# Local attention on one core: keys normalised first, the queries' norm moved into the masking instruction, and the projection copies issued before the fourth exponential

## The chip, the core and the metric

One core of a Trainium2 chip runs the whole program in one launch. The metric is device time in microseconds (us), taken as the median of a few executions; one further execution was recorded by the hardware profiler. All lines (L1134 and so on) are lines of the kernel before, unless the text says otherwise.

## The reference, cut to what matters

The program is a chain of four blocks on an input of 2 batches of 2048 tokens with 256 channels: causal attention, a quantised linear layer, a second causal attention, and then two layers of *local attention followed by a feed-forward network*. Only local attention is touched:

```python
qkv = shift_token(x) @ wqkv              # 256 -> 3 x 512, 8 heads of 64
q, k = l2norm(q) * qs, l2norm(k) * ksc   # each head's vector over its length
q, k = rotary_xpos(q, k)                 # x * cos + rotate_half(x) * sin, per position
# 16 windows of 128 tokens; a window's queries see its own keys and those of the window before
sim = einsum(8 * q, k); sim = where(mask, -big, sim)
x = x + (softmax(sim) @ v) @ wo
```

The norm of a query is one number per token and head, so it can be multiplied in before the scores are made or after. The tables of cosines and sines are ready in SBUF when the stage begins.

## The kernel before, in words

`local_attention` (L1134 to L1484) runs four times in an execution: 2 batches by 2 layers. Each run works through 16 windows of 128 tokens (`w`), and in each window through 4 pairs of heads (`p`); `n = 4w + p` numbers the 64 pairs. Each engine has its own instruction list, written out by hand, and runs it strictly in that order; semaphores (`S[...]`) join the lists. While window `w` is attended, window `w+1` is projected, rotated, normalised and transposed.

- **TensorE** (L1178 to L1281). For each pair: `scores` (L1217), then work for the window ahead, then `turn_p(n-1)` (L1225, transposes of the probabilities of the pair before) and `pv(n-2)` (L1237, probabilities times values). The work ahead is: at p = 0 `turn_h` (L1187) and the projections of queries and keys (L1197); at p = 2 the projection of values; at p = 3 first `out(w-1)` (L1252, the output projection) and then `turn_qk(w+1)` (L1206), which transposes the normalised queries `qn` and keys `kn` into the PSUM banks BQ and BK.
- **ScalarE** (L1283 to L1356). `exp(n)` (L1320) for each pair; at p = 0 `h_out` and the squares of both projections (L1300); at p = 2 `v_take`; at p = 3, after `exp(n)`, `qk_out(w+1)`: the copy of the transposed queries (L1308) and two copies of the keys into their block layout (L1314). Then `p_out(n-1)` (L1326), and at p = 1 `o_out(w-1)` (L1330).
- **VectorE** (L1382 to L1483). `maximum` (L1437, adds the mask to the scores, writes them out and takes the row's extreme), `scale` (L1446 reciprocal, L1449 multiplication), and for the window ahead `squares` (L1399 sum, L1402 clamp), `rotate` (L1415 cosine part, L1418 sine part), `normalise` (L1427, product with the inverse norm, for `qn` and `kn`) and `add` (L1455).
- **GpSimd** (L1358 to L1380). For queries and then keys: the inverse norm as a power (L1376, 128 x 8 values), and the sum of the cosine and sine parts (L1378, in place in `prod_cos`). In layer 0 it also keeps a copy of x (L1371).

The first scores of a window wait for both copies of its keys (L1213), so TensorE can't begin window `w+1` before `qk_out(w+1)` is done. `PROJECTED` (L1147) says at which pair each projection is issued, for TensorE and ScalarE alike.

Of the kernel before, what the change touches and what calls it, by code (L numbers as in the profile page):

```python
# [25 lines left out]
P = 128  # L26
# [1107 lines left out]
def local_attention(k, l, x2, F, keep):  # L1134
# [7 lines left out]
              "sq_q sq_k rot_q rot_k sumsq sum_q sum_k inv_n qn kn q_T k_T q_T_out k_T_out scored maxed exped rinv pn "  # L1142
# [4 lines left out]
    PROJECTED = ((0, 1), (), (2,), ())  # L1147
    with ExitStack() as ctx:
# [7 lines left out]
        ssum, inv_n, mhalf = sb("ssum", [P, 2 * LH]), sb("inv_norm", [P, 2 * LH]), sb("mhalf", [P, 2 * LH])  # L1156
        qn, kn = sb("qn", [P, INNER]), sb("kn", [P, INNER])
# [12 lines left out]
        with nc.Block() as block:  # L1170
# [8 lines left out]
            def _(pe):  # L1179
# [21 lines left out]
                def turn_qk(w):  # L1201

                    for src, bank, ready, done in ((qn, BQ, "qn", "q_T"), (kn, BK, "kn", "k_T")):
                        pe.wait_ge(S[ready], w + 1)
                        for p in range(NP):
                            ins = pe.transpose(ps[:, bank, p * P:(p + 1) * P], src[:, p * P:(p + 1) * P], identf[:, :])  # L1206
                        ins.then_inc(S[done], 1)
# [49 lines left out]
                for i, come in enumerate(("w_q", "w_k", "w_v")):  # L1257
                    pe.wait_ge(early[come], 16)
                    project(0, i)
# [3 lines left out]
                for n in range(PAIRS + 2):  # L1263
                    w, p = n // NP, n % NP
                    if n < PAIRS:
                        scores(n)
                        if p == 0 and w + 2 < NT:
                            turn_h(w + 2)
                        if w + 1 < NT:
                            for i in PROJECTED[p]:  # L1270
                                project(w + 1, i)
                        if p == 3:
                            if w:
                                out(w - 1)
                            if w + 1 < NT:
                                turn_qk(w + 1)
                    if 1 <= n <= PAIRS:
                        turn_p(n - 1)
                    if n >= 2:
                        pv(n - 2)  # L1280
# [3 lines left out]
            def _(act):  # L1284
# [47 lines left out]
                h_out(0)  # L1332
                square(0, 0)
                square(0, 1)
# [3 lines left out]
                for n in range(PAIRS + 1):  # L1338
                    w, p = n // NP, n % NP
                    if n < PAIRS:  # L1340
                        exp(n)
                        if p == 0 and w + 2 < NT:
                            h_out(w + 2)
                        if w + 1 < NT:
                            for i in PROJECTED[p]:
                                if i < 2:
                                    square(w + 1, i)
                                else:
                                    v_take(w + 1)
                            if p == 3:  # L1350
                                qk_out(w + 1)
# [7 lines left out]
            def _(pool):  # L1359
# [9 lines left out]
                for w in range(NT):  # L1369
                    if l == 0 and w:  # L1370
                        pool.tensor_copy(keep[:, w - 1, :], x[:, w, :]).then_inc(S["kept"], 1)  # L1371
                    for i, rotated in enumerate(("rot_q", "rot_k")):
                        own = slice(i * LH, (i + 1) * LH)

                        pool.wait_ge(S["clamp"], 2 * w + i + 1)
                        pool.tensor_tensor(inv_n[:, own], ssum[:, own], mhalf[:, own], ALU.pow).then_inc(S["inv_n"], 1)  # L1376
                        pool.wait_ge(S[rotated], w + 1)
                        pool.tensor_tensor(pc[:, i, :], pc[:, i, :], psn[:, i, :], ALU.add).then_inc(S["sumsq"], 1)  # L1378
# [4 lines left out]
            def _(dve):  # L1383
# [20 lines left out]
                def rotate(w, i, parts=(0, 1)):  # L1404
# [3 lines left out]
                    dve.wait_ge(S["kn"], w)  # L1408
# [12 lines left out]
                def normalise(w):  # L1421
                    dve.wait_ge(S["k_T"], w)
                    for i, (dst, done) in enumerate(((qn, "qn"), (kn, "kn"))):
                        dve.wait_ge(S["inv_n"], 2 * w + i + 1)
                        dve.wait_ge(S["sumsq"], 2 * w + i + 1)
                        r3 = inv_n[:, i * LH:(i + 1) * LH].rearrange("p (h o) -> p h o", o=1).to_broadcast([P, LH, LD])
                        dve.tensor_tensor(dst[:, :].rearrange("p (h d) -> p h d", h=LH),  # L1427
                                          pc[:, i, :].rearrange("p (h d) -> p h d", h=LH), r3, ALU.mult)\
                            .then_inc(S[done], 1)

                def maximum(n):
                    w = n // NP
# [3 lines left out]
                    for h in range(2):  # L1436
                        ins = dve.tensor_tensor_reduce(out=pr[:, n % 2, h, :], in0=ps[:, BS + n % 2, h * 2 * P:(h + 1) * 2 * P],  # L1437
                                                       in1=m, scale=1.0, scalar=3e38, op0=ALU.add, op1=ALU.min,
# [19 lines left out]
                for i in range(2):  # L1458
                    squares(0, i)
                dve.wait_ge(early["tab_ready"], 4)  # L1460
                for i in range(2):
                    rotate(0, i)
                normalise(0)
                dve.wait_ge(S["masks"], 6)
                for n in range(PAIRS):
                    w, p = n // NP, n % NP
                    ahead = w + 1 < NT
                    if p == 1 and ahead:
                        squares(w + 1, 1)
                    maximum(n)  # L1470
                    if p == 1 and ahead:
                        rotate(w + 1, 1, (0,))
                    scale(n)
                    if p == 1 and ahead:
                        rotate(w + 1, 1, (1,))
                    if p == 0 and ahead:
                        squares(w + 1, 0)
                        rotate(w + 1, 0)
                    if p == 2 and ahead:
# [278 lines left out]
```

## Time and profile before

| | us |
|---|---|
| median of 3 executions | 4344.6 (4340.57 to 4346.11) |
| the profiled execution, its own time | 4337.45 |
| its span in the trace | 4335.9 |
| the four runs of local attention in it | 1277.7 to 1593.5, 1737.0 to 2051.1, 3417.3 to 3733.5, 3877.2 to 4189.9: together 1258.8 |
| TensorE busy over the whole span | 3800.3 (88%) |
| VectorE, ScalarE, GpSimd busy | 2902.3 (67%), 2045.6 (47%), 895.6 (21%) |
| mean granted TensorE clock | 0.934 of full rate |

Engines in the profile are named PE (matmul), PEld (TensorE's weight load), DVE (VectorE), ACT (ScalarE), POOL (GpSimd) and SP (SyncE). A group row gives line, engine, operation, output<-inputs, shapes and count, then after the bar the busy time in us and the mean duration in ns, and after the second bar the idle time of the engine before these instructions and who ended it. A timeline row gives start and duration in us. Small negative distances between neighbours on one engine are pipelining.

### The profile page before, as it was taken

Reading aid. Unit: us, or ns where it says so; the run is one execution under the profiler, and the core shown is the slowest. Engines: PE = TensorE matmul, PEld = TensorE weight load, DVE = VectorE, ACT = ScalarE, POOL = GpSimd, SP = SyncE. Lnnn points to the kernel's source line nnn. Section 1 sums busy time; section 2 is a strip of 40 time slices with the busy share of each in tenths; the row PEclk is TensorE's granted clock in tenths of the full one; section 3 lists DMA queues with packets and bytes.
Section 4 is the critical chain, followed back from the end, with each engine's and each line's share of the span. In section 5 each row is a group of like instructions: output and inputs, shape, how many; then the busy total and the mean of one; then the engine's idle time right before and its main releaser. Section 6 shows DMA issues by size and latency. Waiting matters only on the chain. (4 is left out here: it accounts for less than half of the span.)

```text
span 4335.9 us, 60351 instructions
## 1 busy us (share of the span) xinstructions
PE 3800.3 (88%) x19732; PEld 1809.3 (42%) x19732; DVE 2902.3 (67%) x7113; ACT 2045.6 (47%) x3685; POOL 895.6 (21%) x804
## 2 busy tenths in 40 slices
PE   7899978899978989898969999679999699888988
PEld 6233334233334545454543333343333355454545
DVE  3989766889756652666349896759896566436653
ACT  2366642366645541455124666324666455315541
POOL 1201013101023321332140010150010333213322
PEclk7799988799989999999988999788999899999999
DMA  3222002222010010000032220022220100100000
GB/s 78 44 31 31 1 2 49 33 30 31 1 62 6 1 49 7 22 6 1 25 69 30 31 31 1 2 51 30 31 31 1 62 6 1 50 26 6 1 10 25
DMA packets 129552, 108.89 MB, mean 25 GB/s; under 512 B 40872, under 2 KB 122320, under 8 KB 128208
## 3 DMA queue, kind: packets, MB, share of 16 engines
q1 hardware_dynamic: 129232, 104.92, 11.9%
q8 instruction: 164, 2.69, 0.3%
q14 instruction: 156, 1.28, 0.1%
HBM read 41.15 MB, written 4.19 MB: 10 GB/s over the span
## 5 line engine op out<-in xcount | busy, mean ns | idle before, releaser
L722 ACT ACTIVATE probs<-banks 128x1024 f32<-128x1024 f32 (+3 forms) x1280 | 1081.2, 895 | 755.2 <-PE banks L690 752.4
L761 DVE TENSOR_REDUCE chunk_max<-banks 128x1 f32<-128x512 f32 (+2 forms) x1728 | 1102.7, 684 | 72.3 <-PE banks L648 53.5
L648 PE MATMUL banks<-stack_k,stack_q 96*128 96x512 bf16 (+3 forms) x2560 | 824.9, 376 | 80.8 <-PEq L142 44.4
L690 PE MATMUL banks<-stack_q,stack_k 99*128 99x512 bf16 (+3 forms) x2560 | 661.6, 350 | 18.6 <-ACT probs L722 18.6
L667 PE MATMUL banks<-probs,values 128*17 128x512 f32 (+3 forms) x5120 | 591.8, 534 | 20.4 <-ACT probs L722 17.0
L648 PEld LDWEIGHTS banks<-stack_k,stack_q 96*128 96x128 bf16 x2560 | 241.2, 99 | 727.0 <-DVE chunk_max L761 402.2
L615 POOL TENSOR_SCALAR_AFFINE_SELECT probs<-probs 128x512 f32<-128x512 f32 x256 | 162.7, 635 | 1669.5 <-ACT probs L722 1666.3
L1320 ACT ACTIVATE probs_l<-probs_l,nmax 128x256 f32<-128x256 f32 x512 | 255.8, 500 | 454.6 <-DVE nmax L1437 454.6
L1217 PE MATMUL banks<-k_blocks,qT 128*128 128x512 f32 x512 | 291.5, 652 | 109.3 <-issue 103.8
L1197 PE MATMUL banks<-wqkv,hT 128*128 128x512 f32 x768 | 366.3, 616 | 2.7 <-issue 2.7
L690 PEld LDWEIGHTS banks<-stack_q,stack_k 99*128 99x128 bf16 x2560 | 232.4, 98 | 279.4 <-ACT probs L722 100.5
L1376 POOL TENSOR_TENSOR inv_norm<-ssum,mhalf 128x8 f32<-128x8 f32 x128 | 210.8, 1647 | 659.0 <-DVE ssum L1402 652.6
L1607 PE MATMUL banks<-hnT,w 128*128 128x512 f32 x704 | 313.6, 606 | 3.5 <-ACT hnT L1630 3.5
L756 DVE CUSTOM_DVE_ANT_0 masked_scores<-banks,wide_mask 128x384 f32<-128x384 f32 (+1 forms) x512 | 299.7, 617 | 17.5 <-PE banks L648 13.7
L1437 DVE CUSTOM_DVE_ANT_0 probs_l<-banks,later_keys 128x256 f32<-128x256 f32 x512 | 195.1, 418 | 118.6 <-PE banks L1217 118.6
L1636 ACT ACTIVATE gelu<-banks,b 128x512 f32<-128x512 f32 x80 | 55.0, 687 | 359.5 <-PE banks L1607 359.5
L1197 PEld LDWEIGHTS banks<-wqkv,hT 128*128 128x128 f32 x768 | 148.4, 200 | 168.9 <-issue 166.6
L1446 DVE RECIPROCAL rinv<-rsum 128x2 f32<-128x2 f32 x256 | 42.6, 166 | 260.5 <-ACT probs_l L1320 260.5
L1685 DVE SCALAR_TENSOR_TENSOR hidden<-banks,b,gelu 128x512 f32<-128x512 f32 x96 | 71.7, 749 | 205.6 <-ACT gelu L1636 197.6
L1607 PEld LDWEIGHTS banks<-hnT,w 128*128 128x128 f32 x704 | 136.9, 195 | 171.5 <-issue 165.8
L1618 PE MATMUL banks<-w,hidden 128*128 128x256 f32 x768 | 173.2, 386 | 14.9 <-DVE hidden L1685 14.9
L1378 POOL TENSOR_TENSOR prod_cos<-prod_cos,prod_sin 128x512 f32<-128x512 f32 x128 | 162.5, 1269 | 106.9 <-DVE prod_sin L1418 106.9
(188 smaller groups left out, 4865.7 us busy)
## 6 DMA issues: line engine op xcount, KB each, us to landing
stack_q<-parts SPq DMA_DIRECT2D x384, 64.0 KB, 2.4
stack_k<-parts SPq DMA_DIRECT2D x384, 64.0 KB, 2.4
xpos<-in_c_xpos SPq DMA_DIRECT2D x4, 2048.0 KB, 8.5
wqkv<-in_L_ffn_wqkv SPq DMA_DIRECT2D x12, 512.0 KB, 11.4
w<-in_L_ffn_w SPq DMA_DIRECT2D x16, 320.0 KB, 3.2
x_tok<-in_L_attn_x SPq DMA_DIRECT2D x8, 512.0 KB, 5.6
rope<-in_c_rope SPq DMA_DIRECT2D x2, 2048.0 KB, 7.6
hs_f<-x_mid SPq DMA_DIRECT2D x16, 256.0 KB
```

Of the source, the lines that this page charges most:

```text
L648: ins = pe.matmul(out, sq[0:KS, c, j0 + j, i * P:(i + 1) * P], sk[0:KS, cc, j0 + j, 0:width], start=True, stop=not (diag and heads > 1), s ...
L667: ins = pe.matmul(ps[32 * j:32 * j + VW, PV, off:CH], values[:, kt, g * GH + j, :], probs[:, s % 2, j, off:CH], start=(kt == 0), stop=(s i ...
L690: ins = pe.matmul(ps[:, SCORE + j, off:CH], keys, sq[0:KS + PARTS, c, j, off:CH], start=True, stop=True, skip_group_check=True)
L722: act.activation(probs[:, s % 2, 2 * half:2 * half + 2, off:CH], ps[:, SCORE + 2 * half:SCORE + 2 * half + 2, off:CH], ACT.Exp)\
L756: dve.tensor_tensor_reduce(out=unread[:, at % 2, 0:width], in0=bank[:, 0:width], in1=wide_mask[:, CH - width:CH], scale=1.0, scalar=-3e38, ...
L761: dve.tensor_reduce(chunk_max[:, n % 2, j:j + heads, i, cc], bank[:, 0:heads * width].rearrange("p (h n) -> p h n", h=heads), AX.X, ALU.ma ...
L1197: ins = pe.matmul(ps[:, bank, :], hT[:, w % 2, t, 1 - t:P + 1 - t], wqkv[:, t, i * INNER:(i + 1) * INNER], start=(t == 0), stop=(t == KT - 1))
L1217: pe.matmul(ps[:, BS + n % 2, :].rearrange("p (a b n) -> p a b n", a=2, b=2), qT[:, p, :], kbd[:, p, :, s0:s1 + 1:s1 - s0, :], start=True, ...
L1320: ins = act.activation(pr[:, n % 2, h, :], pr[:, n % 2, h, :], ACT.Exp, bias=nmax[:, n % 2, h:h + 1], scale=-1.0, accum_out=rsum[:, n % 2, ...
L1376: pool.tensor_tensor(inv_n[:, own], ssum[:, own], mhalf[:, own], ALU.pow).then_inc(S["inv_n"], 1)
L1437: ins = dve.tensor_tensor_reduce(out=pr[:, n % 2, h, :], in0=ps[:, BS + n % 2, h * 2 * P:(h + 1) * 2 * P], in1=m, scale=1.0, scalar=3e38, ...
L1607: ins = pe.matmul(ps[:, bank + n % 2, :], w1[:, t, at:at + P], hT[:, t, :], start=(t == 0), stop=(t == KT - 1))
```

## The change

1. **TensorE**: the keys are projected before the queries; at p = 3 `turn_qk(w+1)` stands before `out(w-1)`; it transposes the unnormalised sum `prod_cos[:, 0]` in place of `qn` and waits for that sum.
2. **VectorE**: `qn` and its multiplication are gone. The queries' inverse norm enters `maximum` as the per-partition operand `scale` in place of the constant 1.0. Squares and rotation of the keys come at p = 0, the rotation of the queries around `maximum` and `scale` of p = 1, `normalise` (keys only) at the end of p = 1, the squares of the queries between `maximum` and `scale` of p = 2.
3. **GpSimd**: power and sum of the keys, sum of the queries, then power of the queries (into one of two buffers).
4. **ScalarE**: keys' squares before queries'; at p = 3 `qk_out(w+1)` stands before `exp(n)` rather than after it.

```diff
-    PROJECTED = ((0, 1), (), (2,), ())
+    PROJECTED = ((1, 0), (), (2,), ())
...
-        ssum, inv_n, mhalf = sb("ssum", [P, 2 * LH]), sb("inv_norm", [P, 2 * LH]), sb("mhalf", [P, 2 * LH])
-        qn, kn = sb("qn", [P, INNER]), sb("kn", [P, INNER])
+        ssum, mhalf = sb("ssum", [P, 2 * LH]), sb("mhalf", [P, 2 * LH])
+        inv_q, inv_k = sb("inv_norm_q", [P, 2, LH]), sb("inv_norm_k", [P, LH])
+        kn = sb("kn", [P, INNER])
...
-                    for src, bank, ready, done in ((qn, BQ, "qn", "q_T"), (kn, BK, "kn", "k_T")):
+                    for src, bank, ready, done in ((pc[:, 0, :], BQ, "q_sum", "q_T"), (kn, BK, "kn", "k_T")):
...
-                for i, come in enumerate(("w_q", "w_k", "w_v")):
+                for i, come in ((1, "w_k"), (0, "w_q"), (2, "w_v")):
...
                         if p == 3:
+                            if w + 1 < NT:
+                                turn_qk(w + 1)
                             if w:
                                 out(w - 1)
-                            if w + 1 < NT:
-                                turn_qk(w + 1)
...
+                square(0, 1)
                 square(0, 0)
-                square(0, 1)
...
                     if n < PAIRS:
+                        if p == 3 and w + 1 < NT:
+                            qk_out(w + 1)
                         exp(n)
...
-                            if p == 3:
-                                qk_out(w + 1)
...
+                    q, kk = slice(0, LH), slice(LH, 2 * LH)
+
+                    pool.wait_ge(S["clamp"], 2 * w + 1)
+                    pool.wait_ge(S["kn"], w)
+                    pool.tensor_tensor(inv_k[:, :], ssum[:, kk], mhalf[:, kk], ALU.pow).then_inc(S["inv_n"], 1)
+                    pool.wait_ge(S["rot_k"], w + 1)
+                    pool.tensor_tensor(pc[:, 1, :], pc[:, 1, :], psn[:, 1, :], ALU.add).then_inc(S["k_sum"], 1)
+                    pool.wait_ge(S["rot_q"], w + 1)
+                    pool.tensor_tensor(pc[:, 0, :], pc[:, 0, :], psn[:, 0, :], ALU.add).then_inc(S["q_sum"], 1)
+                    pool.wait_ge(S["clamp"], 2 * w + 2)
+                    if w >= 2:
+                        pool.wait_ge(S["maxed"], NP * (w - 1))
+                    pool.tensor_tensor(inv_q[:, w % 2, :], ssum[:, q], mhalf[:, q], ALU.pow).then_inc(S["inv_n"], 1)
...
                 def normalise(w):
                     dve.wait_ge(S["k_T"], w)
+                    dve.wait_ge(S["inv_n"], 2 * w + 1)
+                    dve.wait_ge(S["k_sum"], w + 1)
+                    r3 = inv_k[:, :].rearrange("p (h o) -> p h o", o=1).to_broadcast([P, LH, LD])
+                    dve.tensor_tensor(kn[:, :].rearrange("p (h d) -> p h d", h=LH),
+                                      pc[:, 1, :].rearrange("p (h d) -> p h d", h=LH), r3, ALU.mult).then_inc(S["kn"], 1)
...
+                    if p == 0:
+                        dve.wait_ge(S["inv_n"], 2 * (w + 1))
...
-                                                       in1=m, scale=1.0, scalar=3e38, op0=ALU.add, op1=ALU.min,
+                                                       in1=m, scale=inv_q[:, w % 2, 2 * p + h:2 * p + h + 1], scalar=3e38, op0=ALU.add, op1=ALU.min,
...
-                    if p == 1 and ahead:
-                        squares(w + 1, 1)
                     maximum(n)
                     if p == 1 and ahead:
-                        rotate(w + 1, 1, (0,))
+                        rotate(w + 1, 0, (0,))
+                    if p == 2 and ahead:
+                        squares(w + 1, 0)
                     scale(n)
+                    if p == 0 and ahead:
+                        squares(w + 1, 1)
+                        rotate(w + 1, 1)
                     if p == 1 and ahead:
-                        rotate(w + 1, 1, (1,))
-                    if p == 0 and ahead:
-                        squares(w + 1, 0)
-                        rotate(w + 1, 0)
-                    if p == 2 and ahead:
+                        rotate(w + 1, 0, (1,))
                         normalise(w + 1)
```

## Rows read from the trace of the kernel before

**Rows 1.** The page, busy time by engine over the whole span.
```profile
PE 3800.3 (88%) x19732; PEld 1809.3 (42%) x19732; DVE 2902.3 (67%) x7113; ACT 2045.6 (47%) x3685; POOL 895.6 (21%) x804
```

**Rows 2.** Busy time in the fourth local-attention stage, and TensorE's own idle there.
```profile
3877.00:4190.00 313.00, 273.40 (x1376) 154.50 (x1376) 205.04 (x662) 167.13 (x465) 97.31 (x68) 0.98 0.04 10
L1217 PE MATMUL banks<-k_blocks,qT 128*128 128x512 f32 x128 | 72.3, 647 | 27.3 <-issue 26.0 <-ACT k_blocks L1314 1.4
```

**Rows 3.** Timeline of one window of that stage, TensorE from p = 0.
```profile
3988.53 1.10 PE L1217 MATMUL banks<-k_blocks,qT 128*128 128x512 f32 x2 [1.73 <-issue]
...
3994.24 1.12 PE L1217 MATMUL banks<-k_blocks,qT 128*128 128x512 f32 x2
...
4000.21 1.13 PE L1217 MATMUL banks<-k_blocks,qT 128*128 128x512 f32 x2
4001.17 1.89 PE L1252 MATMUL banks<-wo_l,oT_l 128*128 128x256 f32 x8
4002.96 0.66 PE L1206 MATMUL banks<-identf,qn 128*128 128x128 f32 x4
4003.56 0.66 PE L1206 MATMUL banks<-identf,kn 128*128 128x128 f32 x4
...
4004.59 0.66 PE L1237 MATMUL banks<-probs_T,v_windows 128*64 128x128 f32 x8
4006.97 1.10 PE L1217 MATMUL banks<-k_blocks,qT 128*128 128x512 f32 x2 [1.73 <-issue]
```

**Rows 4.** Groups of that stage on ScalarE, VectorE and GpSimd, costliest first.
```profile
L1320 ACT ACTIVATE probs_l<-probs_l,nmax 128x256 f32<-128x256 f32 x128 | 63.9, 500 | 113.3 <-DVE nmax L1437 113.3
...
L1437 DVE CUSTOM_DVE_ANT_0 probs_l<-banks,later_keys 128x256 f32<-128x256 f32 x128 | 48.8, 418 | 29.1 <-PE banks L1217 29.1
...
L1378 POOL TENSOR_TENSOR prod_cos<-prod_cos,prod_sin 128x512 f32<-128x512 f32 x32 | 40.6, 1270 | 26.4 <-DVE prod_sin L1418 26.4
L1449 DVE TENSOR_SCALAR probs_l<-probs_l,rinv 128x256 f32<-128x256 f32 x128 | 39.5, 351 | 2.2
...
L1418 DVE TENSOR_TENSOR prod_sin<-banks,xpos 128x256 f32<-128x256 f32 x64 | 23.9, 416 | 0.0
...
L1415 DVE TENSOR_TENSOR prod_cos<-banks,xpos 128x512 f32<-128x512 f32 x32 | 21.9, 686 | 0.0
...
L1314 ACT COPY k_blocks<-banks 64x512 f32<-64x512 f32 x32 | 18.5, 578 | 2.5 <-PE banks L1206 2.2
```

**Rows 5.** Two whole-trace lines (min/median/max ns): a product with a per-partition operand; a copy.
```profile
L526 DVE TENSOR_SCALAR vbuf<-banks,qscale x32: 750/751/751, 75.8 to 2259.6; 128x512 f32<-128x512 f32 x32
...
L474 DVE COPY values<-banks x16: 677/692/692, 85.5 to 2862.2; 128x512 f32<-128x512 f32 x16
```

**Rows 6.** Whole-trace lines (min/median/max ns): clamp L1402, and the pair L535, L558.
```profile
L1402 DVE TENSOR_SCALAR ssum<-ssum x128: 170/173/1108, 1284.5 to 4161.1; 128x8 f32<-128x8 f32 x128
...
L535 DVE TENSOR_TENSOR rbuf<-vbuf,parts x64: 680/693/1465, 78.2 to 2909.7; 128x512 f32<-128x512 f32 x64
...
L558 POOL TENSOR_TENSOR parts<-rbuf,parts x64: 1144/1157/1714, 79.7 to 2911.4; 128x512 bf16<-128x512 f32 x64
```

**Rows 7.** Timeline of the fourth stage's start: GpSimd's power beside VectorE, and the first scores.
```profile
3888.09 1.65 POOL L1376 TENSOR_TENSOR inv_norm<-ssum,mhalf 128x8 f32<-128x8 f32 x1
3888.27 0.69 DVE L1427 TENSOR_TENSOR qn<-prod_cos,inv_norm 128x512 f32<-128x512 f32 x1 [0.22 <-POOL prod_cos L1378]
...
3891.82 1.11 PE L1206 MATMUL banks<-identf,kn 128*128 128x128 f32 x4 [1.62 <-DVE kn L1427]
```

**Rows 8.** Timeline of that stage's first window: a maximum of p = 1, and two holes.
```profile
3904.04 0.41 DVE L1437 CUSTOM_DVE_ANT_0 probs_l<-banks,later_keys 128x256 f32<-128x256 f32 x1
...
3906.83 0.66 PE L1225 MATMUL banks<-identf,probs_l 128*128 128x128 f32 x4 [1.66 <-DVE probs_l L1449]
...
3910.75 0.66 PE L1206 MATMUL banks<-identf,qn 128*128 128x128 f32 x4 [1.62 <-DVE qn L1427]
```

**Rows 9.** Busy time and granted clock (third from last) in one of three spells.
```profile
2014.00:2019.00 5.00, 4.64 (x7) 2.03 (x8) 1.56 (x7) 2.03 (x7) 0.00 (x0) 0.66 0.00 0
```

More of the change, by code:

```diff
@@ L1141, in local_attention @@
     S = Stage(nc, k["pool"], "kept masks zero_x halves zero_k h_T h_T_out qk_q qk_k v_mm v_out "
-              "sq_q sq_k rot_q rot_k sumsq sum_q sum_k inv_n qn kn q_T k_T q_T_out k_T_out scored maxed exped rinv pn "
+              "sq_q sq_k rot_q rot_k q_sum k_sum sum_q sum_k inv_n kn q_T k_T q_T_out k_T_out scored maxed exped rinv pn "
               "p_T p_T_out pv o_T_out y x_out clamp")
@@ L1371, in _ @@
                         pool.tensor_copy(keep[:, w - 1, :], x[:, w, :]).then_inc(S["kept"], 1)
[L1372 to L1378, printed above, removed]
+                    q, kk = slice(0, LH), slice(LH, 2 * LH)
[10 more added lines that the diff above has]
+                    pool.tensor_tensor(inv_q[:, w % 2, :], ssum[:, q], mhalf[:, q], ALU.pow).then_inc(S["inv_n"], 1)
                 if l == 0:
@@ L1407, in rotate @@
                     dve.wait_ge(S[squared], w + 1)
-                    dve.wait_ge(S["kn"], w)
+                    dve.wait_ge(S["kn" if i else "q_T"], w)
                     src = ps[:, bank, :].rearrange("p (h d) -> p h d", h=LH)
@@ L1422, in normalise @@
                     dve.wait_ge(S["k_T"], w)
[L1423 to L1429, printed above, removed]
+                    dve.wait_ge(S["inv_n"], 2 * w + 1)
[3 more added lines that the diff above has]
+                                      pc[:, 1, :].rearrange("p (h d) -> p h d", h=LH), r3, ALU.mult).then_inc(S["kn"], 1)
                 def maximum(n):
-                    w = n // NP
+                    w, p = n // NP, n % NP
+                    if p == 0:
+                        dve.wait_ge(S["inv_n"], 2 * (w + 1))
                     m = later[:, 0 if w == 0 else 1 if w % SLOT == 0 else 2, :]
@@ L1456, in add @@
                                       ALU.add).then_inc(S["x_out"], 1)
-                for i in range(2):
+                for i in (1, 0):
                     squares(0, i)
                 dve.wait_ge(early["tab_ready"], 4)
-                for i in range(2):
+                for i in (1, 0):
                     rotate(0, i)
```

## The prediction

> **What bounds the kernel now.** The page comes first: TensorE is busy 88% of the span [rows 1]. That is a mean over unlike stages, so the stage is read next. In the fourth of the four local-attention stages TensorE works 273.4 of 313 us, VectorE 205.0, ScalarE 167.1 and GpSimd 97.3. Nearly all that TensorE lacks stands in one group, the scores: 27.3 us of idle before them [rows 2]. The view by group is so far only a sum; the timeline of one window shows how it is made. Scores of p = 0 start at 3988.53 and those of the next window at 4006.97, a period of 18.44 us, and in it TensorE has one hole, 1.73 us before the window's first scores [rows 3]. I counted these holes in the four stages: 15 in each, 60 in all, each 1.73 us. "Issue" as releaser hides the cause, and the order in the code gives it: the first scores wait for both key copies on ScalarE. Those copies start when `exp` of p = 3 is over, and that one waited for the third and fourth scores, which on TensorE stood in front of the output projection and the transposes. So the loop is bound by TensorE's work plus a detour over ScalarE.
>
> **The walk through a window after the change.** I set time 0 at the start of the window's first scores and shift the recorded distances. All times here are for full clock.
>
> *TensorE.* Its work is the same instructions; two blocks swap. The fourth scores start at 4000.21, which is +11.68, and the next block +12.64 [rows 3]. The two transposes take 0.60 each start to start, so the queries are turned by +13.30 and the keys by about +13.90. Then come the output projection (1.79 to the next start), the transposes of p = 2 and the values' product, and TensorE is through at +16.71 (4004.59 + 0.66 less 3988.53) as before.
>
> *ScalarE.* The query copy and the two key copies (0.58 each [rows 4]) run from +13.3 and from +13.9, so the keys are in place at about +15.2. TensorE wants them at +16.6: the hole is closed with 1.4 us to spare. What is late next is `exp` of p = 3: it starts at +15.1 in place of about +13.7 and ends at +16.2 (two of 0.50 and a read-out). Behind it on ScalarE stands only the copy of the probabilities of p = 2, needed by a product in the next window; behind it through VectorE stands `scale` (two of 0.35 and a reciprocal), done by +17.0, and the sum `add`, done by +17.4. The next maximum can begin only when its scores end, at +17.7, and the transposes that need these probabilities come after 5 us of projections. So the delay costs nothing; without that cover it would be 1.4 us a window.
>
> *VectorE.* The maximum of p = 1 follows its scores, which end at +6.83 [rows 3]; before it stand the keys' sums and rotation, done at +6.3. The queries' cosine part (0.69) lies beside the exponential, `scale` ends at +9.75, the sine part (two of 0.42, less their overlap) at +10.4, the keys' product (0.69) at +11.0, the maximum of p = 2 at +11.8, and the squares of the queries fit where VectorE waits for the exponential [rows 4]. The removed product `qn` (0.69 a window) and the clamp that once took 1.1 us (below) lie beside TensorE's work, so they bring nothing themselves.
>
> *The per-partition operand.* No row shows this masking instruction with one. Nearest are a product from PSUM with such an operand, 751 ns, and a copy from PSUM of the same size, 692 ns [rows 5]: a difference of 59 ns. Between 0 and 0.06 us an instruction I take 0.06, or 0.12 a maximum. Less than nothing is excluded, as it does the same elements. It is already in the walk.
>
> *GpSimd.* The queries' sum is now what TensorE waits for. It can start when the sine part ends, +10.5, takes 1.27 [rows 4], and is wanted at +12.6. But at that moment VectorE is in the keys' product, which also reads two operands from SBUF. The trace has such a pair elsewhere: the VectorE difference L535 takes 693 ns at the median and up to 1465, and GpSimd's L558 1157 and up to 1714 [rows 6], whichever came second being the long one. So I add 0.5 us: the sum is ready at +12.3, 0.3 before it is wanted. Without such blocking it would be +11.8. The Trainium skill ("SBUF — State Buffer", Who interferes with whom) says that a VectorE instruction with two SBUF inputs and a GpSimd instruction that reads SBUF shut each other out for the whole instruction; the trace agrees by L535 and L558.
>
> The queries' power (1.65) now lies beside `scale` of p = 2. In the start-up `qn` ran its usual 0.69 inside such a power [rows 7], so I add nothing. The other end of the bound is a full wait as the clamp shows it, 170 to 1108 ns, for GpSimd's sum [rows 6]: the power from +12.7 to +14.35 would hold `scale` back from +13.9 to +15.0, and TensorE turns these probabilities at +15.6, so either end costs nothing. By the same section of the skill the power would shut `scale` out; the trace does not bear that out for `qn`, and no row shows it for `scale`.
>
> The keys' clamp meets an idle GpSimd after the change, and the queries' one, due at +12.5, a sum that ends at +12.3. The new wait of the first maximum for the queries' power is met early (+14.4 against +17.7).
>
> **The sum.** Holes: back to back, the scores begin 0.07 before the product before them ends, so each of the 60 gives 1.73 + 0.07 = 1.80, together 108. *First window* of each stage: there is no output projection yet, and two more holes of 1.66 and 1.62 [rows 8] come from the late maximum and late `qn`. With the keys rotated first, the maximum of p = 1, now at 3904.04, starts 1.5 earlier, at the end of the keys' rotation, and the first hole goes; the second is mostly gone, as the queries' sum is ready about 0.3 after the fourth scores. But then ScalarE holds the key copies back (exponential, value copy and probability copy stand before them), and by the same walk I get the second window's scores 1.9 earlier beyond the 1.80: 4 x 1.9 = 7.6. *Start-up*: the keys were turned at 3891.82 [rows 7], after the queries' power and the keys' sum one after the other on GpSimd (1.65 + 1.27). Now both sums follow each other, the queries' one runs from 3888.1 to 3889.4, the queries are turned to 3890.6 and the keys after them: 1.2 earlier, 4 x 1.2 = 4.8. *Clock*: in three places, each just after such a hole, the granted clock fell to the lower level, 1.2 GHz (0.66 over 5 us is 1.7 us of full-rate time lost) [rows 9]. All other holes saw no fall, so the link is weak, but without the hole TensorE did not pause: I count 3 x 1.5 = 4.5. DMAs are not touched.
>
> Sum: 108 + 7.6 + 4.8 + 4.5 = 125 us. The profiled execution took 4337.45, so its like would take 4212.5. The median of the runs is 7.2 us above the profiled one; part of that may be more such clock spells, which the change would remove as well. Between 4212 and 4220 I take 4217.
>
> **The rivals.**
> 1. *The queries' sum comes late.* My spare time is 0.3 us a window. A masking instruction dearer by more than 0.06, or GpSimd starting only after the keys' product and the next maximum (0.77), would turn it into a wait of 0.3 to 1.1 us at each of 60 windows: 18 to 66 us, giving 4235 to 4283. For it: L558 did lengthen by 0.55. Against: the maximum reads one operand from PSUM and such an instruction never shows a lengthening beside GpSimd. Chance 0.15.
> 2. *The order pays nothing*: the clock. Were a spell of half rate to follow each window's eight transposes and take 1.7 us, 60 x 1.7 = 102 us would go again, 4319 or so. Against: the transposes of the probabilities stand all through these windows and three spells at 60 holes are all there were. The Trainium skill ("TensorE: Matmul & The Clock Gate", Transpose) says that transposes do not count as busy the same way for the clock; this trace bears it out at most in these three. Chance 0.03. If the operand changed nothing and nothing moved, the time would be that of before, within 0.2% (which is about what a measurement of this kernel can tell from no change); the hole is too plain for more than 0.02.
> 3. *Slower.* The masking instruction with a per-partition operand becomes much slower. It stands twice before the queries' sum and eight times in a window. The gain is 125/60 = 2.1 us a window; a wait of 2.1 + 0.3 = 2.4 us for the sum eats it, so it decides at 1.2 us more for each of the two. At four times today's 0.42 (+1.7 with the overlap, 3.4 before the sum) the time is (3.4 - 2.4) x 60 = 60 us above before, 4400. Nothing in the trace resembles that. Chance 0.03.
>
> **How the numbers follow.** The forecast has 0.77. Its own bounds: start-up and first windows worth nothing and no clock spell saved, 4344.6 - 108 = 4237; a few us more for cheaper operands or a median that loses its spells, 4205. The first rival's lower half reaches 4260. So the range is 4205 to 4260. Faster 0.95, same 0.02, slower 0.03.
>
> **What would show it.** In the changed profile: a window period of 16.6 to 16.7 us; no idle over 0.1 us in front of a window's first scores beyond the stage's start; the four stages shorter by 31 each; ScalarE idle before the key copies ending on the keys' transposes; the masking instruction at 0.42 to 0.48; GpSimd's queries' sum at 1.7 to 1.8 in place of 1.27, ending before the transposes. A wait of the query transposes on the queries' sum would show rival 1; the granted clock of these stages below 0.97, rival 2.

## The result, and the profile after

The changed kernel takes 4229.2 us in the median of four executions (4227.19 to 4233.28), against 4343.11 for the kernel before: a ratio of 0.9739, with a 95% interval of 0.9725 to 0.9754. It is 113.9 us faster; 4217 us was forecast, with a range of 4205 to 4260. The profiled execution took 4233.28 us for a span of 4231.3.

| four local-attention stages together, us | before | after | gained |
|---|---|---|---|
| start of a stage to its first scores | 71.0 | 64.8 | 6.2 |
| first window | 82.8 | 64.4 | 18.4 |
| second window | 73.8 | 65.1 | 8.7 |
| third to fourteenth window (48 in all) | 888.2 | 816.0 | 72.2 |
| fifteenth window | 74.7 | 64.3 | 10.4 |
| last window and end | 68.2 | 71.2 | -3.0 |
| all | 1258.7 | 1145.8 | 112.9 |

A window is counted from its first scores (L1217 before, L1218 after) to those of the next. The steady period fell from 18.44 to 17.00 us, where 16.64 was forecast. The rest of the program is unchanged. It took 3085.5 us in this profiled execution against 3077.1 in that of before, and 3075.4 in a further one of the changed kernel (experiment 0), so nothing systematic lies there; the medians gained 113.9.

The page of the changed kernel, busy time by engine, and then the busy times of its fourth stage, as in [rows 1, 2] (columns: stretch, length, busy us and count of PE, PEld, DVE, ACT, POOL, granted clock, DMA share, GB/s):

```profile
PE 3778.0 (89%) x19732; PEld 1808.6 (43%) x19732; DVE 2843.5 (67%) x7049; ACT 2050.9 (48%) x3685; POOL 919.6 (22%) x804
```
```profile
3799.00:4086.00 287.00, 269.08 (x1376) 155.06 (x1376) 190.13 (x646) 168.47 (x465) 103.20 (x68) 0.98 0.04 11
```

TensorE's idle time in the stage fell from 39.6 to 17.9 us; VectorE's busy time fell from 205.0 to 190.1: the 16 products `qn` (11) and the 15 waits of the clamp (0.93 each, 14) are gone, and against that the 128 masking instructions take 8 more and the start-up's product of the keys 1 more, which leaves 16 where the busy time shows 14.9. The groups of that stage:

```profile
L1218 PE MATMUL banks<-k_blocks,qT 128*128 128x512 f32 x128 | 72.7, 650 | 1.7 <-ACT k_blocks L1315 1.4 <-issue 0.3
L1444 DVE CUSTOM_DVE_ANT_0 probs_l<-banks,later_keys,inv_norm_q 128x256 f32<-128x256 f32 x128 | 56.6, 480 | 17.7 <-PE banks L1218 17.7
L1381 POOL TENSOR_TENSOR prod_cos<-prod_cos,prod_sin 128x512 f32<-128x512 f32 x16 | 26.0, 1625 | 41.5 <-DVE prod_sin L1425 41.5
L1188 PE MATMUL banks<-identf,x_tok 128*128 128x128 f32 x32 | 6.7, 293 | 9.5 <-DVE x_mid L1462 6.2 <-PEq L142 3.3
```

The 27.3 us of idle in front of the scores [rows 2] are 1.7 now. In their place stands a wait that the prediction did not have: `turn_h` (L1188) waits 6.2 us in this stage for VectorE's `add` (L1462), 12 times 0.52 us. The timeline of one window's end shows what leads there (start, duration, engine, line; the rows of TensorE's other work left out):

```profile
3926.57 0.68 DVE L1433 TENSOR_TENSOR kn<-prod_cos,inv_norm_k 128x512 f32<-128x512 f32 x1
...
3926.73 1.65 POOL L1381 TENSOR_TENSOR prod_cos<-prod_cos,prod_sin 128x512 f32<-128x512 f32 x1 [2.95 <-DVE prod_sin L1425]
3927.16 0.48 DVE L1444 CUSTOM_DVE_ANT_0 probs_l<-banks,later_keys,inv_norm_q 128x256 f32<-128x256 f32 x1
...
3928.09 0.51 ACT L1321 ACTIVATE probs_l<-probs_l,nmax 128x256 f32<-128x256 f32 x1 [2.00 <-DVE nmax L1444]
...
3928.79 0.60 PE L1207 MATMUL banks<-identf,prod_cos 128*128 128x128 f32 x4
3928.94 1.65 POOL L1385 TENSOR_TENSOR inv_norm_q<-ssum,mhalf 128x8 f32<-128x8 f32 x1 [0.56 <-DVE ssum L1409]
...
3929.09 0.56 ACT L1305 COPY v_windows<-banks 128x512 f32<-128x512 f32 x1
...
3929.22 0.60 PE L1207 MATMUL banks<-identf,kn 128*128 128x128 f32 x4
3929.42 0.62 DVE L1456 TENSOR_SCALAR probs_l<-probs_l,rinv 128x256 f32<-128x256 f32 x2
3929.56 0.58 ACT L1327 COPY probs_T<-banks 128x512 f32<-128x512 f32 x1
3929.66 1.89 PE L1253 MATMUL banks<-wo_l,oT_l 128*128 128x256 f32 x8
...
3930.03 0.59 ACT L1309 COPY qT<-banks 128x512 f32<-128x512 f32 x1
...
3930.51 1.19 ACT L1315 COPY k_blocks<-banks 64x512 f32<-64x512 f32 x2
...
3931.72 0.51 ACT L1321 ACTIVATE probs_l<-probs_l,nmax 128x256 f32<-128x256 f32 x1
...
3932.51 1.13 PE L1218 MATMUL banks<-k_blocks,qT 128*128 128x512 f32 x2
...
3932.85 0.17 DVE L1453 RECIPROCAL rinv<-rsum 128x2 f32<-128x2 f32 x1 [2.01 <-ACT probs_l L1321]
3933.05 0.62 DVE L1456 TENSOR_SCALAR probs_l<-probs_l,rinv 128x256 f32<-128x256 f32 x2
3933.59 0.42 DVE L1462 TENSOR_TENSOR x_mid<-banks,x_tok 128x256 f32<-128x256 f32 x1
...
3934.15 0.41 PE L1188 MATMUL banks<-identf,x_tok 128*128 128x128 f32 x2 [0.52 <-DVE x_mid L1462]
```

From 3928.09 on ScalarE has no pause: exponential of p = 2, value copy, probability copy, query copy, two key copies, exponential of p = 3, until 3932.8. Then VectorE scales and only then does `add`; then `turn_h` starts; with it the projections and the second scores, on which the maximum of p = 1 waits, then VectorE's work up to the maximum of p = 2, and the round closes. TensorE, which set the pace but for its hole, now runs inside this loop. The key copies are done at 3931.7, 0.8 before the scores that need them.

### The profile page after: what moved, and what is told of

The parts are those of the page before. It is cut to its first block and busy times, and to the rows that moved or that the text cites. A ratio compares the mean times of both kernels' runs of the same rounds, so it can differ in the third digit from the quotient of the medians.

```text
span 4231.3 us, 60343 instructions
## 1 busy us (share of the span) xinstructions
PE 3778.0 (89%) x19732; PEld 1808.6 (43%) x19732; DVE 2843.5 (67%) x7049; ACT 2050.9 (48%) x3685; POOL 919.6 (22%) x804
## 5 line engine op out<-in xcount | busy, mean ns | idle before, releaser
L1218 PE MATMUL banks<-k_blocks,qT 128*128 128x512 f32 x512 | 290.8, 650 | 6.7 <-ACT k_blocks L1315 5.5
L1444 DVE CUSTOM_DVE_ANT_0 probs_l<-banks,later_keys,inv_norm_q 128x256 f32<-128x256 f32 x512 | 226.3, 480 | 71.0 <-PE banks L1218 70.8
L1377 POOL TENSOR_TENSOR inv_norm_k<-ssum,mhalf 128x8 f32<-128x8 f32 x64 | 104.8, 1638 | 436.8 <-DVE ssum L1409 427.9
L1624 PE MATMUL banks<-w,hidden 128*128 128x256 f32 x768 | 173.4, 386 | 14.9 <-DVE hidden L1691 14.9
L1226 PEld LDWEIGHTS banks<-identf,probs_l 128*128 128x128 f32 x1024 | 126.2, 141 | 123.1 <-issue 77.3
```

The costliest lines, as they stand in the source:

```text
L1218: pe.matmul(ps[:, BS + n % 2, :].rearrange("p (a b n) -> p a b n", a=2, b=2), qT[:, p, :], kbd[:, p, :, s0:s1 + 1:s1 - s0, :], start=True, ...
L1624: ins = pe.matmul(ps[:, BY + i % 2, 0:C], hid[:, n, i * P:(i + 1) * P], w2[:, n, :], start=(n == 0), stop=(n == NHT - 1))
```

## The experiments

Theory A, after the trace: the period of 17.0 us is this loop, and `turn_h` waits for `add` (the code has it wait for `x_out`, the semaphore that `add` of the window before raises). Rival B: the hole is TensorE's own or another engine's. About the gain itself there were two views too: that the orders at p = 3 brought it, or that the earlier keys and queries did. The kernel before ran beside all of them: 4336.9 in the first four, 4338.1 in the next four, 4337.8 in the last three. All ratios are to it.

**0. The changed kernel again**, unaltered, as the mark for the others.

> The changed kernel itself, unaltered, on the same chip as the experiments, so that they can be set against it. Runs of the kernel before were 6 us lower in the first four experiments (4336.9), so 0.9739 x 4337 = about 4224 if this is the same chip or 4229 if not; period 17.0 us, hole of 0.52 us in front of turn_h.

Measured: 4228.8 us, ratio 0.9750 (0.9737 to 0.9764). By this ratio it would stand at 4228.5 beside the first four.

**1. The sum in front of scale.**

```diff
+                    if p == 3 and w:
+                        add(w - 1)
                     scale(n)
...
-                    if p == 3 and w:
-                        add(w - 1)
```

> The changed kernel, but VectorE does the sum with the residual (add) of p = 3 in front of scale instead of behind it; nothing else moves. The changed kernel's trace has a hole of 0.52 us on TensorE in front of turn_h, 12 in each stage, and a window period of 17.0 us. Theory A (turn_h waits for add, and add stands behind the scale that follows the delayed fourth exponential): the output projection is ready about 2.4 us before that add, and VectorE idles 2.0 us there, so the hole goes, the period becomes 16.6 to 16.7, and the time is 4229 - 13 x 4 x 0.36 = about 4210. Theory B (turn_h waits for something else, such as ScalarE's copies of hT, or the hole is TensorE's own): hole and time stay, 4226 to 4232.

Measured: 4192.65 us, ratio 0.9667 (0.9651 to 0.9683); period 16.29. VectorE in a window of this kernel, and TensorE in the same window:

```profile
3912.14 0.42 DVE L1462 TENSOR_TENSOR x_mid<-banks,x_tok 128x256 f32<-128x256 f32 x1 [0.75 <-PE banks L1253]
3913.41 0.17 DVE L1453 RECIPROCAL rinv<-rsum 128x2 f32<-128x2 f32 x1 [0.84 <-ACT probs_l L1321]
```
```profile
3909.34 0.60 PE L1207 MATMUL banks<-identf,prod_cos 128*128 128x128 f32 x4
3909.77 0.60 PE L1207 MATMUL banks<-identf,kn 128*128 128x128 f32 x4
3910.21 1.89 PE L1253 MATMUL banks<-wo_l,oT_l 128*128 128x256 f32 x8
...
3913.06 1.12 PE L1218 MATMUL banks<-k_blocks,qT 128*128 128x512 f32 x2
3914.02 0.38 PE L1188 MATMUL banks<-identf,x_tok 128*128 128x128 f32 x2
```

`add` sits in the pause in which VectorE waits for the exponential anyway, and TensorE has no hole left. Theory A holds. The gain was underestimated, 36 us instead of 19: the period went not to 16.64 but to 16.29. The stage lengths in the traces (1145.8 to 1114.0) say 32. So the stop in front of `turn_h` had cost 0.71 us a window from start to start, more than the 0.52 of idle that the profile puts there. The 0.35 between 16.64 and 16.29 comes out block by block. The transposes follow each other here at 0.43 and 0.44, where the kernel before shows 0.60 [rows 3] and 0.49, and the output projection takes 1.73 to the next start in place of 1.79: together 0.28. In that trace `kn` ended at 4003.51 and its transposes began at 4003.56, so they were waiting just in time, and I had taken that spacing for their price. Another 0.10 had been lost in the same way on the transposes of the probabilities of p = 1, and the start of the window goes 0.03 the other way.

**2. ScalarE's order undone** (`qk_out` behind the fourth exponential, as before).

```diff
-                        if p == 3 and w + 1 < NT:
-                            qk_out(w + 1)
                         exp(n)
...
+                            if p == 3:
+                                qk_out(w + 1)
```

> The changed kernel with ScalarE's order alone undone: qk_out stands behind the fourth exponential again. By my walk the keys' copies end at +18.1 instead of +16.2 after the first scores, 1.2 to 1.5 us after TensorE wants the next window's first scores, and the hole in front of turn_h goes, as the exponential and add are early again. Period 17.5 to 17.8, time 4229 + 56 x (0.5 to 0.8) = 4257 to 4274. Rival (the copies were early enough anyway once keys come first and turn_qk precedes out): no hole at the scores, time 4210 to 4230.

Measured: 4268.17, ratio 0.9842 (0.9825 to 0.9858); period 17.38. One window of it:

```profile
3945.27 0.66 PE L1238 MATMUL banks<-probs_T,v_windows 128*64 128x128 f32 x8
3946.96 1.10 PE L1218 MATMUL banks<-k_blocks,qT 128*128 128x512 f32 x2 [1.04 <-issue]
```

The hole is back in front of the first scores and gone in front of `turn_h`. ScalarE's order is worth 0.0092 of the time, 40 us. The period is below the 17.5 that I expected, and the time met its range for another reason: the steady windows lose only 0.38 each, 18 us in the 48 from the third on, while in the trace the first two windows of the four stages lose 24 us together. About 10 us of that are spells at the lower clock level, one in each stage at a hole of 2.1 us in front of the second window's first scores (in the fourth, 0.51 over 3858.9 to 3862.3).

**3. TensorE's order undone** (the output projection in front of the transposes).

```diff
                         if p == 3:
+                            if w:
+                                out(w - 1)
                             if w + 1 < NT:
                                 turn_qk(w + 1)
-                            if w:
-                                out(w - 1)
```

> The changed kernel with TensorE's order at p = 3 alone undone: the output projection stands in front of the transposes again. The keys are turned 1.75 us later, so the copies, the fourth exponential behind them, scale and add are later by about 1.0 (some of it is slack on ScalarE): period 18.0, holes in front of both the first scores and turn_h, time 4229 + 56 x 1.0 = about 4285. Rival (the order of TensorE's blocks pays little, as ScalarE reaches the query copy only at +14.5 anyway): 4230 to 4245.

Measured: 4289.57, ratio 0.9890 (0.9873 to 0.9906); period 18.11, both holes as expected:

```profile
3943.44 1.10 PE L1218 MATMUL banks<-k_blocks,qT 128*128 128x512 f32 x2 [0.34 <-issue]
3945.78 0.41 PE L1188 MATMUL banks<-identf,x_tok 128*128 128x128 f32 x2 [1.25 <-DVE x_mid L1462]
```

This order is worth 0.0140 of the time, 61 us.

**4. No per-partition operand** (`scale=1.0`; the queries' norm is left out of the scores).

```diff
-                                                       in1=m, scale=inv_q[:, w % 2, 2 * p + h:2 * p + h + 1], scalar=3e38, op0=ALU.add, op1=ALU.min,
+                                                       in1=m, scale=1.0, scalar=3e38, op0=ALU.add, op1=ALU.min,
```

> The changed kernel with scale=1.0 in the masking instruction in place of the per-partition operand: this leaves the queries' norm out of the scores. The instruction goes from 0.48 back to 0.42 us. If the loop that sets the period runs through VectorE (maxima of p = 1 and p = 2, then ScalarE, add, turn_h), two maxima of two instructions each stand in it: 4 x 0.06 = 0.24 us a window, period 16.76, time 4229 - 13 = 4216, and the hole shrinks to about 0.28. If TensorE or another engine sets the period, time and hole stay.

Measured: 4212.76, ratio 0.9716 (0.9700 to 0.9733); period 16.75, `turn_h` idle 0.27 us 12 times. The four instructions in the loop are worth 0.25 us a window. This confirms in a second way that the loop runs through VectorE.

**5. The two orders alone, in the kernel before.**

```diff
                         if p == 3:
+                            if w + 1 < NT:
+                                turn_qk(w + 1)
                             if w:
                                 out(w - 1)
-                            if w + 1 < NT:
-                                turn_qk(w + 1)
...
+                        if p == 3 and w + 1 < NT:
+                            qk_out(w + 1)
                         exp(n)
...
-                            if p == 3:
-                                qk_out(w + 1)
```

> The kernel before with only the two swaps at p = 3: turn_qk in front of the output projection on TensorE, qk_out in front of the fourth exponential on ScalarE. Queries' product, keys' place and the masking instruction stay as they were. Theory (the swaps need the keys and queries early): the keys' product ends 2.1 us after the fourth scores, TensorE waits there 1.6 to 2.1 us instead of in front of the first scores, so the period stays at 18.1 to 18.5 and the time within 4315 to 4345. Rival (the swaps are the whole change and the rest is decoration): period about 17.0 and 4225 to 4240.

Measured: 4333.04, ratio 0.9986 (0.9977 to 0.9995); period 18.40:

```profile
3980.79 0.66 PE L1206 MATMUL banks<-identf,qn 128*128 128x128 f32 x4 [1.63 <-DVE qn L1427]
3981.39 0.66 PE L1206 MATMUL banks<-identf,kn 128*128 128x128 f32 x4
```

The hole of 1.73 in front of the scores has become one of 1.63 in front of the transposes. Without earlier keys and queries the orders bring 0.0014 of the time, some 6 us. Even of that some 4 us is no shorter path: the trace of the kernel before has three spells at the lower clock (1.48, 1.48 and 1.38 us), and this one has none in its windows.

**6. The keys' product behind the maximum of p = 2.**

```diff
                         rotate(w + 1, 0, (1,))
-                        normalise(w + 1)
...
                     if p == 2 and ahead:
+                        normalise(w + 1)
                         squares(w + 1, 0)
```

> The changed kernel with the keys' product (normalise) moved from the end of p = 1 to behind the maximum of p = 2. Loop theory (maximum of p = 2, its exponential, value copy, probability copy, key copies, fourth exponential, scale, add, turn_h set the period of 17.0): the maximum and all behind it start 0.6 us earlier, so the period falls to 16.4 to 16.5 and the time by 25 to 30 us, to about 4200. Blocking theory: GpSimd's sum of the queries now starts beside the maximum, which reads one operand from SBUF, and takes 1.27 us in place of 1.65, and the keys' product, coming second, is lengthened from 0.68 to 1.1 to 1.7 us. Rival (the period is set by TensorE's own instructions or by the key copies): period and time stay.

Measured: 4197.26, ratio 0.9676 (0.9661 to 0.9690); period 16.40. The same two lines over the whole trace, first of the changed kernel, then of this one (min/median/max ns):

```profile
L1433 DVE TENSOR_TENSOR kn<-prod_cos,inv_norm_k x64: 678/682/1669, 1290.9 to 4061.6; 128x512 f32<-128x512 f32 x64
...
L1381 POOL TENSOR_TENSOR prod_cos<-prod_cos,prod_sin x64: 1259/1650/1656, 1290.8 to 4061.8; 128x512 f32<-128x512 f32 x64
```
```profile
L1433 DVE TENSOR_TENSOR kn<-prod_cos,inv_norm_k x64: 1174/1181/1672, 1289.3 to 4028.5; 128x512 f32<-128x512 f32 x64
...
L1381 POOL TENSOR_TENSOR prod_cos<-prod_cos,prod_sin x64: 1261/1276/1282, 1289.1 to 4027.8; 128x512 f32<-128x512 f32 x64
```

The loop is 0.6 us shorter, and what was blocked changed sides: GpSimd's sum is back at its 1.27, and the keys' product takes 1.18 in place of 0.68. Of the pair, the one that starts second is the long one.

**7. The sum in front of scale, and no operand** (the queries' norm is left out).

> The version with add in front of scale, and scale=1.0 in the masking instruction (this leaves the queries' norm out of the scores). If with add early TensorE alone sets the period (16.29 us, no holes), the 0.06 us of the operand lie beside it: period 16.29 and the time of the version with add early, within 3 us. If VectorE still had a part in it, 0.24 us a window less, 13 us.

Measured: 4194.43, ratio 0.9669 (0.9654 to 0.9684); period 16.29. With `add` early the operand costs nothing in a window, as TensorE sets the pace. Only the end of a stage is shorter without it, 17.18 us in place of 17.67, which is too little to be seen in the times.

**8. The queries' norm as a product again**, within the new orders. The main lines:

```diff
-                    for src, bank, ready, done in ((pc[:, 0, :], BQ, "q_sum", "q_T"), (kn, BK, "kn", "k_T")):
+                    for src, bank, ready, done in ((qn, BQ, "qn", "q_T"), (kn, BK, "kn", "k_T")):
...
                     if p == 2 and ahead:
-                        squares(w + 1, 0)
+                        normalise_q(w + 1)
...
                     if p == 0 and ahead:
                         squares(w + 1, 1)
                         rotate(w + 1, 1)
+                        squares(w + 1, 0)
```

> The changed kernel with its new orders, but the queries' norm stays a product of its own (qn, now behind the maximum of p = 2), the masking instruction has scale=1.0 again, the queries' squares are summed at the end of p = 0 where VectorE idled 1.0 us, and GpSimd does the queries' power before their sum. Theory 1 (the gain is in the orders; the norm as a factor only saves 0.69 us of VectorE that was idle anyway): queries are turned about 0.3 us later, ScalarE reaches the query copy at +14.5 anyway, the loop is 0.24 us shorter through the cheaper masking instruction: period 16.75 to 17.0, time 4213 to 4229. Theory 2 (without the factor the queries come too late): TensorE waits 1 us or more before the transposes of qn, period 17.5 or more, time over 4255.

Measured: 4282.50, ratio 0.9874 (0.9858 to 0.9889); period 17.50 in the stages 2 and 4 and 17.59 in 1 and 3. These are the numbers of Theory 2, and TensorE waits in front of the transposes of `qn`. Its row, then GpSimd's sum of the keys and VectorE's clamp in the same window:

```profile
3936.75 0.66 PE L1207 MATMUL banks<-identf,qn 128*128 128x128 f32 x4 [0.89 <-DVE qn L1440]
```
```profile
3929.56 1.27 POOL L1379 TENSOR_TENSOR prod_cos<-prod_cos,prod_sin 128x512 f32<-128x512 f32 x1
```
```profile
3929.75 1.10 DVE L1409 TENSOR_SCALAR ssum<-ssum 128x8 f32<-128x8 f32 x1
```

I had overlooked that the queries' squares, put at the end of p = 0, do not fit VectorE's pause there: their clamp falls beside GpSimd's sum of the keys and takes 1.10 us instead of 0.17 (as in the kernel before [rows 6]), which makes the maximum of p = 1 and all that follows late. It starts at +7.74 after the window's first scores (3930.77 less 3923.03). In the changed kernel it starts at +7.60, of which 0.68 is the stop in front of `turn_h`, so without that stop at +6.92. So some 0.75 of the wait comes from the clamp. From start to start TensorE waits 1.05 here, so only about 0.3 is left for the product that stands between the queries' sum and their transposes, as Theory 1 had it. By this estimate an arrangement without the clamp's wait would have a period of about 16.75, also that of Theory 1; none was run. What is shown is that the factor with its late norm is worth 0.0124 of the time, 54 us, against this one arrangement of the product. It takes the product out of the chain and lets the queries' squares and their norm come later. About half of the 54 us, 26 in the trace, lies in the 48 windows from the third to the fourteenth, and that half goes by the estimate to the place of the squares; 10 lie in the start-ups.

**9 and 10. Both moves, and the start.** Experiment 9 joins the moves of 1 and 6. Experiment 10 also rotates before it sums the queries' squares at a stage's start:

```diff
-                for i in (1, 0):
-                    squares(0, i)
+                squares(0, 1)
                 dve.wait_ge(early["tab_ready"], 4)
                 for i in (1, 0):
                     rotate(0, i)
+                squares(0, 0)
                 normalise(0)
```

> The changed kernel with both moves: add in front of scale at p = 3, keys' product behind the maximum of p = 2. TensorE had no hole left with the first alone (period 16.29), and 0.11 us more a window with the second alone (16.40). If TensorE's own instructions are the floor: period 16.29, the time of the first alone, about 4193, within 3 us. Less than 16.2 would mean that the floor was not TensorE's.

> Both moves, and at a stage's start VectorE rotates keys and queries before it sums the queries' squares (the table is long there). In the changed kernel's start-up TensorE idles 3.66 us before the queries' transposes, as GpSimd's sum of the queries ends late and the keys' product behind it takes 1.67 us. With the rotations 0.86 us earlier both sums come 0.9 to 1.3 us earlier: 4 x 0.9 to 1.3 = 4 to 5 us less than both moves alone, about 4188. Rival (the start-up is held by something else, such as the tables or the first projections): no difference.

Measured: 4194.73, ratio 0.9670 (0.9657 to 0.9683), and 4183.94, ratio 0.9646 (0.9633 to 0.9659). The first shows the floor again, 16.29. The second is the fastest of all. Its start-up, and that of the changed kernel:

```profile
3773.30 0.63 PE L1207 MATMUL banks<-identf,prod_cos 128*128 128x128 f32 x4 [2.26 <-POOL prod_cos L1381]
```
```profile
3811.86 1.09 PE L1207 MATMUL banks<-identf,prod_cos 128*128 128x128 f32 x4 [3.66 <-POOL prod_cos L1381]
```

In this stage, the fourth, the hole is 1.4 shorter, and the same transposes run at 0.63 instead of 1.09. The granted clock was at its upper level there (1.00 over 3773.3 to 3773.8), and at its lower one in the changed kernel (0.50 over 3811.8 to 3813.8), where TensorE had been idle 3.66 us before. From a stage's start to its first scores all four stages together take 56.1 us, against 64.3 in experiment 9. This gives 8 of the 10 us that came where 4 to 5 were expected: 6.6 from the holes, which are 1.4 to 2.1 shorter in the four stages, and the rest from what follows them.

## Why the prediction was right, point by point

- **The bound and its cause: right.** The 60 holes of 1.73 us are gone, and experiments 2, 3 and 5 have one again, in front of the scores or in front of the transposes, by undoing or isolating a part.
- **108 us for the holes: too much.** The 48 windows from the third to the fourteenth gave 1.44 each in place of 1.80, clock spells left out (the second and the fifteenth gave 2.2 each, but they are only 8 in all). Three steps of the walk failed. *ScalarE*: it had the query copy at +13.3 and the keys in place at +15.2, "1.4 us to spare". The value copy and the copy of the probabilities of p = 1 (0.56 and 0.58) stand between the exponential of p = 2 and the query copy, which starts at +14.5 (3930.03 less 3915.51, this window's first scores); the keys are in place at +16.2. Of these 1.2, 0.7 is the new hole, which pushes the round back, and 0.5 the two copies: in experiment 1, which has no hole, the query copy starts at +13.8. I had counted these two copies for the first window and forgotten them for the others. *What is late next*: of the fourth exponential I named the copy of probabilities, `scale`, `add` and the next maximum, and said that the delay costs nothing. The waiter behind `add` was missed: `turn_h` waits for it. It cost 0.71 us a window from start to start, and experiment 1 removed it. *TensorE's floor*: +16.64, by the spacing of transposes that were waiting; the one measured is 16.29. The last error hid half of the others, which was luck. One of the signs named beforehand also stayed away: ScalarE was to idle in front of the key copies until the keys' transposes, and it has no pause there.
- **VectorE's walk: right.** Less the 0.7 of the new hole, `scale` of p = 1 ends at +9.8 (9.75 forecast), the keys' product at +11.0 (11.0) and the maximum of p = 2 at +11.8 (11.8).
- **First window, +7.6 beyond the holes: too little.** It gave 4.6 us each in place of 3.7 (4.4 in the stages 2 and 4). **Start-up, 4.8**: 6.2. In the stages 2 and 4 it was the 1.2 each that the walk gave; in the trace of experiment 0, the same kernel, the four start-ups take 67.3 us in place of 64.8, so a gain of this size varies by some 2 us from one execution to the next. **The end of a stage** was left out and lost 0.75 each, of which the operand is about 0.5 (experiments 1 and 7: 17.67 and 17.18).
- **Clock, 4.5: right in size.** No window of the changed kernel's four stages beyond the start shows a spell; the three of before had cost 1.48, 1.48 and 1.38 against their neighbours. That the holes caused them is not shown. Experiments 3, 5 and 8 have holes of 0.9 to 1.6 us in every steady window and no spell in any of them; experiment 2 has one in each stage, at its longest hole (2.1 us).
- **The per-partition operand: right.** 480 ns in place of 418, where 0.06 was taken. The walk had counted it on VectorE but gave it no cost in the period. Experiment 4 shows that it was not free: it lay in the loop, 0.0034 of the time or 15 us. In the steady windows it is free once TensorE sets the pace (experiment 7).
- **GpSimd's sum: right.** It took 1.65, where 1.77 was forecast, ended at 3928.38 and was wanted at 3928.8. Rival 1 didn't occur; that the time came out between it and the forecast has the other reasons above. The blocking is real: experiment 6 moved it to the other side.
- **The product `qn`, "beside TensorE's work, so they bring nothing themselves": wrong in its sense.** It lay in time in which VectorE was idle anyway. As a link of the chain from the queries' sum to their transposes it can matter: in experiment 8 about 0.3 of TensorE's wait of 1.05 us goes to it (an estimate), and the rest to the place of the queries' squares in that arrangement.
- **The other rivals**: the granted clock did not fall (0.98 in the stage), and the masking instruction did not become much slower.

## What to carry to other kernels

When a hole is closed, follow every waiter of each instruction that is delayed for it, to the end of its engine's list: here a small sum (`add`) behind the delayed work became part of the new bound, and moving it by one place brought 36 us more. An exchange of two blocks pays only if their inputs are ready by then (experiment 5: 6 us alone, 114 with the rest), so the effects of the parts do not add up. The spacing of instructions that wait just in time is not their price: the floor of an engine is read where nothing waits. And when a part is put back to see what it was worth, as in experiment 8, the trace has to show that nothing else became slower with it.

## What the runs showed of the hardware

- GpSimd's power does not hold VectorE back here. In the timeline above `scale` (two instructions in 0.62 us) runs inside a power of 1.65 us; over the whole trace its instructions take 345 to 356 ns, inside a power or not. The other way round the power did wait: in the four start-ups it came behind a product of the keys that was itself held up by the sum, and took 2.10 us in place of 1.65. GpSimd's sum of two operands did hold back the clamp (1.10 in place of 0.17) and, in experiment 6, the keys' product. The Trainium skill ("SBUF — State Buffer", Who interferes with whom) lets whichever starts first hold the port for its whole instruction; the trace agrees for the sums, and for the power only where it came second.
- A blocked pair was slightly cheaper than one after the other. The keys' product and GpSimd's sum started 0.16 apart, and the sum took 0.38 more, not the 0.5 of the walk: 1.81 from the first start to the last end, where 0.68 and 1.27 in a row make 1.95. In the start-ups the product, coming second, took 1.67 in place of 0.68.
- Two groups of four fp32 transposes of 128 x 128 follow each other at 0.43 us when their operands are ready (the keys' product had ended 2 us before), and at 0.60 when the second operand came 0.05 before its transposes; the profile shows no idle in front of the second group.
